# Second FFN's first chunk beside the attention's last group of heads

## What is computed

```python
def _L0_ffn_ref(x, w1, b1, w2, b2):           # 256 -> 1024 -> 256
    h = jnp.einsum('bsd,fd->bsf', x, w1_q) + b1
    h = jax.nn.gelu(h, approximate=False)
    return jnp.einsum('bsf,df->bsd', h, w2_q) + b2

def _L0_attn_ref(x, Wq, bq, Wk, bk, Wv, bv, Wo, bo):
    ...
    scores = jnp.einsum('bhqd,bhkd->bhqk', Q, K) * (1.0 / math.sqrt(D_K))
    scores = jnp.where(causal[None, None], scores, -jnp.inf)
    probs = jax.nn.softmax(scores, axis=-1)
    att = jnp.einsum('bhqk,bhkd->bhqd', probs, V)
    ...
```

## Time and profile before

| | us |
|---|---|
| median of 3 runs | 994.21 |
| lowest, highest | 993.02, 995.79 |
| the profiled execution | 995.83 |
| its span, first to last instruction | 994.6 |

### The profile page before, as it was taken

One profiled execution on the slowest core, in us unless ns is written; L12 is line 12 of the kernel. 1 busy time (PEld: TensorE's weight loads), 2 busy tenths in 40 slices (PEclk: granted clock), 3 DMA queues, 4 the chain that ended last, 5 costly groups with the idle time before them and its releaser, 6 DMA issues. The chain is left out here.

```text
span 994.6 us, 11031 instructions
## 1 busy us (share of the span) xinstructions
PE 726.8 (73%) x3706; PEld 500.3 (50%) x3706; DVE 593.2 (60%) x1008; ACT 373.8 (38%) x757; POOL 311.4 (31%) x370
## 2 busy tenths in 40 slices
PE   2974787788897787699149368599678798676980
PEld 1763554344433667588036245265355454565870
DVE  4974454666721676454348386688868899562333
ACT  3410143345663332033024755666363554121330
POOL 2142032201111301500510055468455677023006
PEclk9997677689986795799559789899979999867995
DMA  4859033020000601354300000000060000103434
GB/s 159 273 58 125 6 58 42 2 33 2 1 1 1 254 1 38 129 188 143 108 14 0 1 0 1 0 1 1 1 254 1 1 0 1 33 33 116 149 117 127
DMA packets 36104, 61.52 MB, mean 62 GB/s; under 512 B 7266, under 2 KB 27106, under 8 KB 34482
## 3 DMA queue, kind: packets, MB, share of 16 engines
q1 hardware_dynamic: 32978, 52.43, 18.8%
q0 software_dynamic: 3072, 8.39, 2.7%
HBM read 35.32 MB, written 17.43 MB: 53 GB/s over the span
## 5 line engine op out<-in xcount | busy, mean ns | idle before, releaser
L1262 PE MATMUL PS<-FB,C 128*128 128x512 f32 x256 | 132.3, 616 | 1.2 <-DVE FB L1896 1.2
L1355 ACT ACTIVATE FA<-PS 128x512 f32<-128x512 f32 (+3 forms) x192 | 80.3, 497 | 71.4 <-PE PS L1037 70.8
L2009 POOL TENSOR_TENSOR FB<-FB,RBF 128x512 f32<-128x512 f32 x51 | 65.7, 1288 | 71.6 <-DVE FB L1887 71.6
L510 PE MATMUL PS<-C,FB 128*128 128x128 f32 x250 | 45.8, 308 | 47.8 <-DVE FB L1558 37.2
L1972 POOL TENSOR_SCALAR_AFFINE_SELECT FA<-FA 128x128 f32<-128x128 f32 x128 | 36.4, 294 | 132.8 <-ACT FA L1355 130.8
L1626 DVE TENSOR_REDUCE FA<-PS 128x2 f32<-128x1024 f32 (+2 forms) x64 | 67.4, 1086 | 11.9 <-PE PS L1016 11.6
L1990 POOL DMA_INDIRECT FB<-GY,FB x32 | 30.7, 959 | 135.9 <-DMA GY<-FB 126.9
L1037 PE MATMUL PS<-RA 64*128 64x512 f32 (+3 forms) x192 | 64.4, 490 | 7.8 <-ACT FA L1355 6.2
L510 PEld LDWEIGHTS PS<-C,FB 128*128 128x128 f32 x250 | 36.3, 161 | 61.1 <-DVE FB L1558 38.5
L1160 PE MATMUL PS<-WE,FB 128*128 x248 | 62.4, 396 | 0.0
L2000 POOL TENSOR_TENSOR FB<-WE,FB 128x512 f32<-128x512 f32 x32 | 42.7, 1336 | 59.4 <-ACT FB L1457 59.4
(11 more groups left out here) (260 smaller groups left out, 1630.6 us busy)
## 6 DMA issues: line engine op xcount, KB each, us to landing
WE<-in_wr SPq DMA_DIRECT2D x8, 1536.0 KB, 11.8
FB<-GX SPq DMA_DIRECT2D x14, 512.0 KB, 4.7
GY<-FB SPq DMA_DIRECT2D x14, 512.0 KB, 3.2
RA<-RA SPq DMA_DIRECT2D x48, 128.0 KB, 4.8
GX<-FA SPq DMA_DIRECT2D x1, 3968.0 KB, 13.9
FA<-in_w SPq DMA_DIRECT2D x2, 1024.0 KB, 7.0
FA<-in_qkvo SPq DMA_DIRECT2D x1, 1536.0 KB, 19.0
FB<-in_we SPq DMA_DIRECT2D x4, 384.0 KB, 3.8
```

The lines of the kernel that those rows point to most:

```text
L510: return pe.matmul(out, in_, ident, start=True, stop=True, is_transpose=True)
L1262: pe.matmul(bank(m), ident, shc[k % 4], start=n == 0, stop=n == DN - 1).then_inc(*yad.inc(ch, n, m))
L1355: act.activation(PT[n % 12][:, c0:], bank(4 + ring_no[(x, *a)] % 3)[:, c0:], ACT.Exp, scale=0.25).then_inc(*exd.inc(*a))
L2009: pool.tensor_tensor(shc[k % 4], sh[k % 5], Cs[(stc.no[ch, n] - 1) % 2], ALU.mult).then_inc(*cma.inc(ch, n, m))
```

## The change

Chunk 0 of the second FFN, with its norm, leaves its place behind the attention. Its norm goes beside the end of the last maxima and the third group of heads, and its `up`s, `down`s and `xadd` are spread in even steps over the last group of heads. The `up`s use banks 2 and 3, the `down`s banks 0 and 1 (two outputs in a bank), the hidden layer four slots in the memory of the query, key and value weights (`Wall`, used as a ring of four where eight slots were), Gelu's output the memory of the rotary tables. `attT(1)` gets fixed banks 4 and 5. `fin`, `attT` and `oproj` of the last group are in the heads' stream. Chunk 1 with its norm follows `oproj(1, 3)`. The number of instructions of each kind on TensorE, VectorE and POOL is the same.

```diff
+def ffn_chunk_steps(u, ch, after=(), aside=()):
+    after, aside = iter(after), iter(aside)
+    yield [("xb", u, ch)]
+    for f in range(8):
+        yield [("up", u, ch, f)]
+        yield next(after, [])
+        yield next(aside, [])
+        if f > 1:
+            yield [("down", u, ch, f - 2)]
+    yield [("down", u, ch, 6), ("down", u, ch, 7), ("xadd", u, ch)]
...
+def second_ffn_steps():
+
+    yield from norm_steps(2, 1)
+    yield from ffn_chunk_steps(1, 1, norm_steps(3, 0))
...
-    yield from by_time([heads, *zeros, *asks, later, maxima], needs)
-    yield [("fin", 1, 3)]
-    yield [("attT", 1)]
-    for i in range(TC):
-        yield [("oproj", 1, i)]
+    needs["stat", 2, 0, 0] = [("oproj", 0, 3)]
+    needs["tr", 2, 0] = [("mtt", 1, 3)]
+    ffn = [seg for seg in chain(norm_steps(2, 0), ffn_chunk_steps(1, 0)) if seg]
+    a, b = ends[1, 3] - 3, over[1, 3]
+    ffn = [(a + (b - a) * k / len(ffn), seg) for k, seg in enumerate(ffn)]
+    heads += [(over[1, 3], [x]) for x in (("fin", 1, 3), ("attT", 1), *[("oproj", 1, i) for i in range(TC)])]
+    yield from by_time([heads, *zeros, *asks, later, ffn, maxima], needs)
...
+        def up_bank(u, ch, f):
+            return bank((2 if (u, ch) == (1, 0) else 4) + f % 2)
+
+        def down_out(u, ch, i):
+
+            return bank(i // 2)[:, i % 2 * D:i % 2 * D + D] if (u, ch) == (1, 0) else bank(i)[:, 0:D]
...
-        for ch in range(NCH):
-            tmp[2, ch], st[2, ch] = [b[:, 0:D] for b in PT[4 * ch:4 * ch + 4]], sts_[ch]
+        tmp[2, 0], st[2, 0] = [b[:, i * D:i * D + D] for b in set0[0:2] for i in range(2)], sts_[0]
+        tmp[2, 1], st[2, 1] = [b[:, 0:D] for b in PT[0:4]], sts_[1]
+        hbuf[1, 0] = [w[:, 0:2048].rearrange("p (f n) -> p f n", f=4) for w in Wall]
+        hs[1, 0] = [FA[:, 4096 + i * CH:4096 + i * CH + CH] for i in range(4)]
...
                     sp.wait_ge(*oxd.at(1, TC - 1))
+                    sp.wait_ge(*dnd.at(1, 0, 7))
...
                     if (s, ch) == (2, 0):
+                        pe.wait_ge(*mtc.at(1, 3))
+                    elif (s, ch) == (2, 1):
                         pe.wait_ge(*rwd.at(1, 3))
                         pe.wait_ge(*oxd.at(1, TC - 1))
...
-                    bk = claim_pair(x, ch)
+                    if ch:
+                        bk = PS[:, 4:6, :]
+                        pe.wait_ge(*exd.at(1, 3, 2 * TC - 1, 3))
+                    else:
+                        bk = claim_pair(x, ch)
...
-                    if ch:
-                        dve.wait_ge(*dnd.at(u, 0, f))
-                    split(Hh[:, f, :], Hl[:, f, :], hs[u][f % 4]).then_inc(*hsp.inc(u, ch, f))
+                    if f >= n:
+                        dve.wait_ge(*dnd.at(u, ch, f - n))
+                    elif (u, ch) == (0, 1):
+                        dve.wait_ge(*dnd.at(0, 0, f))
+                    split(hl[0][:, f % n, :], hl[1][:, f % n, :], hs[u, ch][f % 4]).then_inc(*hsp.inc(u, ch, f))
```

More of the change, by code:

```diff
@@ L117, in norm_steps, with first_ffn_steps @@
     yield [("xn", s, ch, 1)]
[L120 to L124, removed]
-    for ch in range(NCH):
[L126 to L130, removed]
-            if ch:
[L132 to L135, removed]
+def ffn_chunk_steps(u, ch, after=(), aside=()):
[8 more added lines that the diff above has]
+    yield [("down", u, ch, 6), ("down", u, ch, 7), ("xadd", u, ch)]
+def first_ffn_steps():
+    yield from ffn_chunk_steps(0, 0, norm_steps(0, 1))
+    yield from ffn_chunk_steps(0, 1, norm_steps(1, 0), [[("qld",)], [("wq",)], [("wo",)]])
+def second_ffn_steps():
+    yield from norm_steps(2, 1)
+    yield from ffn_chunk_steps(1, 1, norm_steps(3, 0))
 def project_steps(ch, what):
@@ L433, in steps @@
     out += [("abs", 1), ("const",)]
-    for part in (ffn_steps(0), attention_steps(), [[("late",)]], ffn_steps(1), moe_steps(0), mamba_steps(), moe_steps(1)):
+    for part in (first_ffn_steps(), attention_steps(), [[("late",)]], second_ffn_steps(), moe_steps(0), mamba_steps(), moe_steps(1)):
         for seg in part:
@@ L496, in bank, with turned @@
             return PS[:, i, :]
+        def turned(s, ch):
+            if (s, ch) == (1, 1):
+                return pair("tr", 1, 1)
+            first = 2 if (s, ch) == (2, 0) else 6 if s < 3 or (s, ch) == (3, 0) else 4 + 2 * (ch or s == 3)
+            return PS[:, first:first + 2, :]
+        def up_bank(u, ch, f):
+            return bank((2 if (u, ch) == (1, 0) else 4) + f % 2)
+        def down_out(u, ch, i):
+            return bank(i // 2)[:, i % 2 * D:i % 2 * D + D] if (u, ch) == (1, 0) else bank(i)[:, 0:D]
         def xn(k, ch, a=0, b=CH):
@@ L564, in build @@
         oxd = sig("s_att_x", of("oproj"))
-        pair_uses = [x for x in plan if x[0] in ("pj", "vj", "diag", "off", "mtt", "attT") or x == ("tr", 1, 1)]
+        pair_uses = [x for x in plan if x[0] in ("pj", "vj", "diag", "off", "mtt") or x in (("tr", 1, 1), ("attT", 0))]
         pair_no = {x: i for i, x in enumerate(pair_uses)}
@@ L648, in build @@
             tmp[0, ch], st[0, ch] = t0, first.take(40)
-        hbuf, hs = [None, None], [None, None]
+        hbuf, hs = {}, {}
         ra, fa = Area(RA[:, NRA - 8192:], 8192), Area(FA[:, 10600:], NFA - 10600)
-        hbuf[0] = [ra.take(8 * CH).rearrange("p (f n) -> p f n", f=8) for _ in range(2)]
-        hs[0] = [fa.take(CH) for _ in range(4)]
+        hbuf[0, 0] = hbuf[0, 1] = [ra.take(8 * CH).rearrange("p (f n) -> p f n", f=8) for _ in range(2)]
+        hs[0, 0] = hs[0, 1] = [fa.take(CH) for _ in range(4)]
         tmp[1, 0], st[1, 0] = [fa.take(D) for _ in range(4)], fa.take(40)
@@ L691, in build @@
         ra, fa = Area(RB[:, NRA2 - 8192:], 8192), Area(FB[:, 2304:], NFA2 - 2304)
-        hbuf[1] = [ra.take(8 * CH).rearrange("p (f n) -> p f n", f=8) for _ in range(2)]
-        hs[1] = [fa.take(CH) for _ in range(4)]
+        hbuf[1, 1] = [ra.take(8 * CH).rearrange("p (f n) -> p f n", f=8) for _ in range(2)]
+        hs[1, 1] = [fa.take(CH) for _ in range(4)]
         fa.take(4 * D + 80)
@@ L940, in tensor_program @@
                         for k in range(2):
-                            t = turn_over(out[k][:, i * P:i * P + P], tmp[s, ch][i][:, k * P:k * P + P])
+                            t = turn_over(out[:, k, i * P:i * P + P], tmp[s, ch][i][:, k * P:k * P + P])
                             if i == TC - 1:
@@ L961, in tensor_program @@
                         pe.wait_ge(*gel.at(u, 0, 6 + f))
-                    group(bank(4 + f % 2), [(W1Q[:, k, f * P:f * P + P], v) for k in range(2) for v in xn(k, ch)]).then_inc(*upd.inc(u, ch, f))
+                    group(up_bank(u, ch, f), [(W1Q[:, k, f * P:f * P + P], v) for k in range(2) for v in xn(k, ch)]).then_inc(*upd.inc(u, ch, f))
                 elif x == "down":
                     u, ch, f = a
-                    Hh, Hl = hbuf[u]
+                    hl = hbuf[u, ch]
+                    slot = f % hl[0].shape[1]
                     pe.wait_ge(*hsp.at(u, ch, f))
@@ L971, in tensor_program @@
                     for i in range(TC):
-                        t = group(bank(i)[:, 0:D], [(h[:, f, i * P:i * P + P], W2Q[:, f, :]) for h in (Hh, Hl)], start=f == 0, stop=f == 7)
+                        shared = (u, ch) == (1, 0)
+                        t = group(down_out(u, ch, i), [(h[:, slot, i * P:i * P + P], W2Q[:, f, :]) for h in hl],
+                                  start=f == 0 and not (shared and i % 2), stop=f == 7, skip=shared)
                     t.then_inc(*dnd.inc(u, ch, f))
@@ L1317, in scalar_program @@
                     s, ch, k = a
-                    src = bank(7) if (s, ch) == (5, 0) else pair("tr", 1, 1)[:, k, :] if (s, ch) == (1, 1) else \
-                        bank(4 + 2 * (ch or s == 3) + k) if s > 2 and (s, ch) != (3, 0) else bank(6 + k)
+                    src = bank(7) if (s, ch) == (5, 0) else turned(s, ch)[:, k, :]
                     act.wait_ge(*trs.at(s, ch, k))
@@ L1330, in scalar_program @@
                         act.wait_ge(*ldc.at())
-                    act.activation(hs[u][f % 4], bank(4 + f % 2), ACT.Gelu, bias=cst("b1")[:, f:f + 1]).then_inc(*gel.inc(u, ch, f))
+                    act.activation(hs[u, ch][f % 4], up_bank(u, ch, f), ACT.Gelu, bias=cst("b1")[:, f:f + 1]).then_inc(*gel.inc(u, ch, f))
                 elif x == "wq":
@@ L1363, in scalar_program @@
                     ch, = a
-                    bk = pair(x, ch)
+                    bk = PS[:, 4:6, :] if ch else pair(x, ch)
                     act.wait_ge(*att_t.at(ch))
@@ L1578, in vector_program @@
                         xt = X[:, ch * TC + i, :]
-                        t = dve.scalar_tensor_tensor(xt, bank(i)[:, 0:D], 0.5, xt, ALU.mult, ALU.add)
+                        t = dve.scalar_tensor_tensor(xt, down_out(u, ch, i), 0.5, xt, ALU.mult, ALU.add)
                     t.then_inc(*xad.inc(u, ch))
```

15 lines of the change are left out of this document (5 added, 10 removed).

## The result

| | median, us | runs |
|---|---|---|
| before | 993.98 | 20 |
| after | 997.97 | 20 |
| ratio after / before | 1.005 (95%: 1.0033 to 1.0066) | |

The account below looks back on a forecast made before the run. The last group of heads was taken as bound by TensorE at 1.2 GHz, moving to ScalarE after the change. Terms -18.2 + 4.0 + 17.7 + 2.5 = +6.0 us on 994.2 gave 1000.2 us, range 995.5 to 1009.5.

Parts of the forecast that it names:

- The sum of ScalarE: Last group of heads: Exps, Gelus, 16 table loads and lost overlap sum to 41 us, making ScalarE the bound.
- The wait ahead of key tile 7: Near the last group's end, ScalarE waits 2.7 us for scores queued behind two `down`s and a `pv`.
- the walk: ScalarE's and TensorE's queues followed against each other through the last group: first exp to `raw` 45.3 us, +17.7 us.
- What was removed: Second FFN, behind the attention: one steady chunk goes, -18.2 us.
- The third group's additions: Third group of heads: statistics, transposes, `xn` copies and `rstd` add +4.0 us, between 2.2 and 5.
- The statistics: Third group: four pairs between VectorE's reductions, where VectorE is the bound, add 2.2 us ahead of `mx` and `mtt`.
- transposes and `xn` together: Third group: eight `tr` transposes cost 1.1 us at 2.4 GHz; `xn` copies and `rstd` cost 0.7 us.
- The clock: Last group: TensorE's clock falls in the sparse beginning and returns in the denser middle, +2.5 us.
- TensorE at 1.2 GHz throughout: Rival, mixed last group: TensorE becomes the bound at up to 61 us; kernel about 1008 us; chance 0.15.
- No measurable change: Rival: clock stays 2.4 GHz, statistics and transposes find gaps (2.2 instead of 4.0); 994.5 to 997 us; chance 0.13.
- Loads that all hide in waits: Rival, last group: table loads fall into ScalarE's 10.9 us of waits for scores; 984 us; chance 0.04.
- A switch that costs more than its load: Rival, last group: 16 x 1.3 = 21 us come on top of the loads; 1021 us; chance 0.02.

Follow-up runs that it names:

- Relu run: The changed kernel with Relu instead of Gelu in chunk 0 of the second FFN, so no extra table loads: 982.88 us, ratio 0.9899.
- the run with the loads alone: The kernel before with eight one-column Gelus, results unused, among the last group's Exps, adding 16 table loads: 1012.18 us, ratio 1.0178.
- the gaps version: The changed kernel with chunk 0's `up`s and `down`s behind the last Exp, between `fin`, `attT`, `oproj` and chunk 1's norm: 984.12 us, ratio 0.9906.

## Why the prediction was right

**The sum of ScalarE** was the step on which it rested, and it held: 32 Exps 14.1 us and 0.9 of lost overlap (together 14.5 measured), 8 Gelus 5.5 (5.5), 16 loads 20.6 (20.6), ScalarE busy 41 (40.56). The wait ahead of key tile 7, 2.7 us in the walk, was 2.95. First exp to `raw`: 45.3 with the clock at 2.4 GHz throughout, 46.94 measured with 17 us at 1.2. The Relu run shows the loads as the cause, the run with the loads alone shows it from the other side.

**What was removed**, -18.2 us, came out at -18.4.

**The third group's additions** were put at +4.0 and measured +2.5, near the lower end of 2.2 to 5. The statistics were right in kind: `mtt`'s transposes wait for VectorE,

```profile
281.06 0.60 PE L531 MATMUL PS<-C,RA 128*8 128x128 f32 x4 [2.48 <-DVE RA L1672]
```

2.48 us where that wait was 0.68 in the kernel before (+1.8, for 2.2 of statistics). But transposes and `xn` together cost only some 0.7 us and not 1.8, since the stretch behind the maxima has room on every engine. This is the term that was mis-sized: I had added 1.1 us of transposes in full to a stretch whose own row showed TensorE idle for 1.3 of 7.44 us. (Half of 1.94 is 0.97 and not 1.1, as the prediction has it; the eight took 1.09 us at 283.27 in the changed kernel.) The room as the reason is argued from these rows; no run tests it.

**The clock.** It fell in the sparse beginning of the group, where TensorE had been busy for 2.98 of 4.61 us, and came back in the dense middle, where it had been busy without a gap from 303.35 on, as the prediction had it. The row of 293.40 to 307.00 above is that stretch, with ScalarE busy for 13.34 of 13.60 us: there the slow clock costs almost nothing. In a second, short one (320.7 to 324.1) ScalarE was busy for 3.18 of 3.40. What is left over the walk is 46.94 - 45.3 = 1.6 us, where 2.5 was taken for the clock. No run separates the clock's share of it; the one long wait that the walk did not have is the 1.19 us at 309.73, for scores that stood behind a `down`, a `pv` and four transposes just after the slow stretch. Both terms lean the same way, and so the forecast was 2 us above the medians' difference.

**Rivals.** TensorE at 1.2 GHz throughout (1008 us) did not happen: the mean clock was 0.82. No measurable change (994.5 to 997) fell, but narrowly, as the interval of the ratio begins 0.33% above no change. Its price of the third group, +2.2, was nearer to the measured +2.5 than my 4.0; its other half, a clock at 2.4 GHz throughout, did not come true, and the last group grew by 19.3 and not 17.7 us. Loads that all hide in waits (984 us) fell with the run of the loads alone, where 8.3 of 22.7 us did. A switch that costs more than its load fell with the rows above: Gelu starts 0.01 us after its load and the load 0.02 after the Exp. The Trainium skill (ScalarE: Activation LUTs, What ACT_TABLE_LOAD costs) adds a drain of about 1.38 us to each switch; in the sixteen switches of this trace there is none. The Trainium skill (the same page, Rules for kernel authors) says to group such functions by table set and to finish one set before the next. The four runs with all of the FFN in the group bear that out: with 16, 12, 8 and 0 extra loads it took 46.9, 45.4, 38.3 and 30.9 us.

## What to carry to other kernels

Before work is put beside other work, list the functions that ScalarE runs on both sides; if they come from different table sets, each alternation costs two loads of 1.28 us here, and in a group where ScalarE was busy for only half of the time little more than a third of the added time hid in its waits (8.3 of 22.7 us). Put it where only one of the two runs, or batch the calls until the engine's sum falls below the neighbour's. When two engines come out nearly equal in such a sum, expect more than the larger of the two: I had put both at 23 us, TensorE was busy for 27.8, and the group took 32.5. This is one run.

## What the runs showed of the hardware that I had not expected

TensorE's clock with FFN matmuls evenly among the heads and no wait for ScalarE: in the Relu run 2.4 GHz was granted from 218.3 to 324.1 us without a break. Up to 286 us that is so in the kernel before as well; what is new is that it lasts through the whole group, where the heads alone lose it after 4 to 5 us (at 289.48 in the kernel before, at 294.4 in the gaps version). So the mixed group with all of the FFN's matmuls took 30.86 us, only 3.3 us more than the heads alone. The change's idea was sounder than I gave it credit for: without the table loads it would have had the FFN chunk nearly free (3.3 us in the last group and 2.5 in the third, for 17.4 less behind it).
